# Two gate projections moved into the first layer, other tail buffers and another GpSimd order in a three-layer kernel

## The reference

```python
x = x + 0.5 * ffn(layernorm(x), base_W, router_W, lora_A, lora_B)
x = x + mixer(layernorm(x), ...)
x = x + 0.5 * ffn(layernorm(x), base_W, router_W, lora_A, lora_B)

# mixer: 8 groups of 16 heads, head size 64, state 128
proj = h @ in_proj_w.T;  gate, xBC, dt = split(proj)      # gate 8192, xBC 8192 + 2*1024, dt 128
xBC = silu(causal_conv(xBC, 4 taps) + conv_b);  x, B, C = split(xBC)
dt = clip(softplus(dt + dt_bias)); cs = cumsum(-dt * head_rank)   # in chunks of 128 tokens
y = selective_scan(x, B, C, dt, cs) + x * D
out = rmsnorm_per_group(y * silu(gate)) * norm_w @ out_proj_w.T
```

## Time and profile before

| | us |
|---|---|
| median of 3 runs (lowest, highest) | 1545.94 (1545.58, 1546.23) |
| the profiled execution, its own time | 1546.05 |
| its span, first to last instruction | 1544.3 |
| TensorE busy | 1487.0 (96%) |
| VectorE busy | 1289.1 (83%) |
| ScalarE busy | 1163.6 (75%) |
| GpSimd busy | 1055.6 (68%) |

### The profile page before, as it was taken

How to read it: one execution, slowest core, us unless ns; L and a number is a source line. 1 busy time by engine, 2 the same in 40 slices (tenths; PEclk the granted TensorE clock), 3 DMA queues, 4 the chain that set the end, 5 groups by cost and what they waited for, 6 DMA issues and landing times. The chain is left out here.

```text
span 1544.3 us, 24931 instructions
## 1 busy us (share of the span) xinstructions
PE 1487.0 (96%) x7784; PEld 1220.4 (79%) x7784; DVE 1289.1 (83%) x1648; ACT 1163.6 (75%) x2666; POOL 1055.6 (68%) x853
## 2 busy tenths in 40 slices
PE   6979799999999999999999999999999999999988
PEld 4757688888888888888888888788888888888766
DVE  6689787998789987998789987998789977998675
ACT  4468787878878787878878787778877887778741
POOL 3015787578856887578857887578757887588830
PEclk9989899999999999999999999999999999999999
DMA  3026443444434442444434442544434442444301
GB/s 124 1 92 185 164 149 102 151 147 147 141 102 155 151 151 90 151 150 151 144 103 152 147 153 83 165 149 148 135 109 151 150 151 76 167 150 143 101 14 55
DMA packets 165683, 198.81 MB, mean 129 GB/s; under 512 B 21040, under 2 KB 86576, under 8 KB 165296
## 3 DMA queue, kind: packets, MB, share of 16 engines
q1 hardware_dynamic: 165552, 197.22, 39.3%
HBM read 160.98 MB, written 36.18 MB: 128 GB/s over the span
## 5 line engine op out<-in xcount | busy, mean ns | idle before, releaser
L166 PE MATMUL bank<-h_hi,mx_w_hi 128*128 128x512 f32 x1152 | 459.6, 399 | 22.6 <-DVE mx_acc L1531 12.0
L167 PE MATMUL bank<-h_lo,mx_w_hi 128*128 128x512 f32 x1152 | 451.0, 392 | 0.0
L168 PE MATMUL bank<-h_hi,mx_w_lo 128*128 128x512 f32 x1152 | 450.1, 391 | 0.0
L976 DVE SCALAR_TENSOR_TENSOR mx_acc<-bank,mx_cw,mx_acc 128x510 f32<-128x510 f32 (+2 forms) x480 | 353.8, 745 | 46.1 <-ACT mx_acc L961 34.1
L1552 DVE TENSOR_TENSOR mx_mix<-mx_mix,mx_cbt 128x1536 f32<-128x1536 f32 x128 | 263.8, 2066 | 56.0 <-ACT mx_mix L1357 55.9
L1347 ACT ACTIVATE mx_mix<-mx_csb,ncs 128x256 f32<-128x256 f32 x512 | 218.0, 498 | 116.8 <-PE bank L1748 116.8
L166 PEld LDWEIGHTS bank<-h_hi,mx_w_hi 128*128 128x128 f32 x1152 | 217.4, 189 | 75.4 <-issue 13.9
L1246 POOL TENSOR_TENSOR mx_ssum<-mx_ssum,mx_sq 128x512 f32<-128x512 f32 x112 | 152.6, 1383 | 156.9 <-ACT mx_sq L1379 156.9
L1233 POOL TENSOR_TENSOR mx_y<-mx_y,mx_sg 128x512 f32<-128x512 f32 x128 | 247.9, 1957 | 10.5 <-DVE mx_y L1560 10.4
L168 PEld LDWEIGHTS bank<-h_hi,mx_w_lo 128*128 128x128 f32 x1152 | 217.5, 189 | 46.4
L167 PEld LDWEIGHTS bank<-h_lo,mx_w_hi 128*128 128x128 f32 x1152 | 217.8, 189 | 42.6
(11 more groups left out here) (172 smaller groups left out, 2261.4 us busy)
## 6 DMA issues: line engine op xcount, KB each, us to landing
mx_csb<-cs_rows SPq DMA_DIRECT2D x128, 512.0 KB, 4.1
mx_w_raw<-in_w_in SPq DMA_DIRECT2D x144, 256.0 KB, 3.6
x_squares<-mx_th SPq DMA_DIRECT2D x128, 256.0 KB, 2.0
mx_xd<-x_squares SPq DMA_DIRECT2D x512, 64.0 KB, 2.0
mx_wo_raw<-in_w_out SPq DMA_DIRECT2D x64, 256.0 KB, 4.2
...
```

The source lines that it names most:

```text
L166: nc.tensor.matmul(out, w_hi, x_hi, start=first, stop=False)
L167: nc.tensor.matmul(out, w_hi, x_lo, start=False, stop=False)
L168: return nc.tensor.matmul(out, w_lo, x_hi, start=False, stop=last)
L976: self.nc.vector.scalar_tensor_tensor(dst, src[:, :, 0:SEQ - k], self.cw[:, c, TAPS - 1 - k:TAPS - k], dst, ALU.mult, ALU.add).then_inc(s[ ...
```

## The change

There are three parts. **First**, the gate projections of steps 0 and 1 of group 0 (24 matmuls) leave the first pair of the mixer and stand in the first layer, after the last C unit and before `transpose_rows`. Their weight tile 3 is loaded in the first layer by SP behind the conv constants, rounded by ScalarE after the second tanh there, and its remainder is GpSimd's last step in that layer. `project_gate` becomes a method of `InProj`. **Second**, the tanh of units 4 and 5 goes to `th` as well, and units 6 and 7 wait for taps only. This holds in each group. **Third**, GpSimd takes a pair's steps in another order: the remainder of the first tile directly after the first `mask_ahead`, then the second `mask_ahead`, the other remainders, and `sum_squares` last.

```diff
@@ ffn_phase, scalar
                 d.tanh_on_act(act, 1)
+                d.ip.round_w(act, 0, 3)
                 for h in range(2):
                     d.ln_on_act(act, h)
@@ ffn_phase, tensor
                 d.ip.project(pe, 0, 3)
+                for st in range(2):
+                    pe.wait_ge(d.s["v"], st + 1)
+                    d.ip.project_gate(pe, 0, st)
                 for h in range(2):
                     d.transpose_rows(pe, h)
@@ DtPart.sync / gpsimd
         self.ip.load_constants(sp, 0)
+        self.ip.load_w(sp, 0, 3)
-        for w in range(3):
+        for w in range(4):
             self.ip.remainder_w(pool, 0, w)
@@ InProj.project
-            if 4 <= u < 6 or (first(g) and u < 4):
+            if 4 <= u < 8 or (first(g) and u < 4):
@@ InProj.project_gate (moved here), its waits
+        pe.wait_ge(s["wlo"], 1 + WPG * g + w + 1)
+        if st == 0 and not first(g):
+            pe.wait_ge(s["ms"], 1 + g)
+        if not (first(g) and st < 2):
+            pe.wait_ge(s["sg"], 1 + STEPS * g + st - 1)
@@ mixer_phase
-            return m.bank[u % 2][:, :] if u < 2 or u >= 4 else th[:, u % 2, :]
+            return m.bank[u % 2][:, :] if u < 2 or u >= 6 else th[:, u % 2, :]
@@ mixer_phase, sync, ahead of the pairs
-            load_w(3)
@@ mixer_phase, gpsimd, ahead of the pairs, and pair
-            remainder_w(3)
             remainder_w(4)
+                splits = [n for n in weights_split_in(g, j) if n % WPG != 5]
                 mask_ahead(g, 2 * j + 2)
+                remainder_w(splits[0])
+                mask_ahead(g, 2 * j + 3)
+                for n in splits[1:]:
+                    remainder_w(n)
                 if j >= 2:
                     for st in before:
                         sum_squares(g, st)
-                mask_ahead(g, 2 * j + 3)
-                for n in weights_split_in(g, j):
-                    if n % WPG != 5:
-                        remainder_w(n)
@@ mixer_phase, scalar, ahead of the pairs
             keep_bc(0, 0)
-            round_w(3)
             tanh_conv(0, 3)
             round_w(4)
@@ mixer_phase, tensor, pair
-                for st in steps:
-                    project_gate(g, st)
+                if not (first(g) and j == 0):
+                    for st in steps:
+                        ip.project_gate(pe, g, st)
```

24 lines of the change are left out of this document (10 added, 14 removed).

## The result

The changed kernel takes 1529.41 us, median of 4 runs (1528.34 to 1529.77). Runs of the kernel before beside them took 1546.09 us (1545.58 to 1547.9). The ratio is 0.9889, 95% interval 0.9872 to 0.9906: 16.7 us less. The profiled execution has a span of 1527.9 us, against 1544.3.

What follows compares the result with a forecast made beforehand. It took TensorE's mixer waits as the bound, mainly 12.0 us for `silu_conv` and 10.4 us for `remainder_w`. From 1546.05 it took 8.2 for the tails and 7.8 for group 0, giving 1530 us, range 1525 to 1537.

Steps and rivals of the forecast that it cites:

- The tails: Seven tails ahead of unit 6: TensorE's wait for `silu_conv` goes, 1.17 us each, 8.2 us in all.
- The gates in the mixer: Pair (0, 0): 5.6 us of matmuls leave, but `mix_tokens` waits for `scale_even`, so they bring nothing by pair (0, 1).
- The first layer: Gates fill TensorE's holes from 86.0 to 91.6; the layer ends within 0.3 us of before, counted as 0.
- GpSimd's order: Group 0, pairs (0, 3) and (0, 4): earlier remainders shorten TensorE's waits, 7.8 us, bounds 3.8 and 11.
- the middle: Central estimate of group 0's gain from GpSimd's new order: 7.8 us, between bounds of 3.8 and 11.
- All of it comes off: Rival: other engines follow TensorE, so 5.6 + 12.0 + 10.4 us and one slow clock of 1.7 go; 1516, chance 0.05.
- only the first wait: Rival: group 0's chain is later than drawn and only 3.8 us remain there; 1534 us, chance 0.18.
- The tails don't close: Rival: at the tails something unseen is as late as `silu_conv`; 1538 us, chance 0.06.
- Slower: Rival: GpSimd's new wait for ScalarE's rounding delays each of 56 pairs; 1574 us if 0.5 us over, chance 0.03.
- The blocked VectorE: Rival: GpSimd beside the four `make_mix` of pairs (0, 2) and (0, 3) costs 2.7 us; 1532.7, chance 0.04.

Runs made afterwards that it cites:

- no_gates: Changed kernel with the two gate projections and tile 3's load, rounding and remainder back in the mixer's pair (0, 0); 1527.95 us.
- even_first: Changed kernel with ScalarE doing `scale_even` ahead of the tanh of unit 6, in pair (0, 0) alone; 1527.84 us.
- w3_memset: Changed kernel with GpSimd's remainder of tile 3 in the first layer replaced by a fill with zeros that reads nothing; 1527.9 us.
- no_tails: Changed kernel with the tanh of units 4 and 5 back in the banks and units 6 and 7 waiting for `silu_conv`; 1538.22 us.

## Why the prediction was right

The forecast was 1530 us, with 1525 to 1537 as its range; it is 1529.41. The sum was right within 0.6 us, but three of its terms were off, and that they made up for each other is luck.

- **The tails.** The mechanism was right: the bank is free when the taps of unit 4 are done, no other releaser takes the place of `silu_conv`, no wait is left, and the groups from the second on are shorter. The term was too small: 7 x 1.42 = 9.9 us (from unit 6 of group 1 to that of group 2 it was 172.34 us and is 170.93) instead of 8.2. The step that failed is the reading of 1.17 us of idle time out of the earlier trace rows as what there was to win. The distance between starts would have given it, here and at each tail.
- **The gates in the mixer.** They give 0.07 us (no_gates against the changed kernel), forecast 0. The reason was right as well: `mix_tokens` of step 0 was held by `scale_even` (even_first moved it), not by TensorE. In detail, pair (0, 1) was forecast at 127.1 and came at 128.55, with the mixer's start 0.9 later. `mix_tokens` came 0.9 us earlier against the mixer's start (forecast 0.8), but behind 9.46 us of idleness it took 5.33 us, and not 2.95 + 1.7. The slow clock costs 2.5 us there. I had taken its price from the earlier trace rows, where 3.4 us passed at half speed; here it lasted until 129.
- **The first layer.** Forecast within 0.3 us of before; it is 0.44 longer. The transposes came at 91.89 (forecast 91.6) and at 94.37 (forecast 93). The step that failed is "GpSimd, with nothing else to do, takes the remainder": I asked who waits for GpSimd and not who runs beside it. Its subtraction stood in VectorE's way (w3_memset). The rest of the 0.9 us by which the mixer starts later lies ahead of unit 3 and isn't the change's: even_first, with the same first layer, started the mixer at 97.22.
- **GpSimd's order.** Forecast 7.8 us for group 0, measured 7.3, and 7.5 alone. Pair (0, 3) came 59.99 us behind the mixer's first product, against 64.30: 4.3 us earlier, forecast 3.8. `mix_tokens` of step 6 was forecast at 171.1 and came at 171.94, with the mixer's start 0.9 later. Pair (0, 4), forecast at 174.1, came at 176.29; against the mixer's start that is 5.8 us won and not 7.1, and another 1.5 came in pair (0, 4) itself (19.58 us instead of 21.08), which no longer starts with the slow clock. I had left open whether the wait ahead of it would bring the slow clock; in the profiled execution it did (4.35 us instead of 2.86), and in w3_memset and no_tails, behind 3.20 and 3.12 us, it did not. The half microsecond by which the middle was too high is within that. (The middle was also added up wrongly: 7.1 to 8.8 less 0.3 gives 7.65, not 7.8.)
- **The rivals.** "All of it comes off" is refused by the gates, whose 5.6 us brought 0.07, and "only the first wait" by pair (0, 4), which came 5.8 us earlier with no wait for L925. "The tails don't close" is refused by the first fence above. "Slower" is refused by groups 1 to 7: no wait for a remainder at all, with GpSimd's new wait for ScalarE's rounding (3.40 us at 172.96) hidden. "The blocked VectorE" did not come at the place that I named: the `make_mix` of pairs (0, 2) and (0, 3) took 2.12, 1.75, 2.13 and 1.75 us, against 2.42 and 1.75 in the earlier trace rows. It came where I had not looked, in the first layer (1.0 us of VectorE, 0.4 of the whole), and in pair (0, 0), where the kernel before had it too.
